# Edge scores: the attributes laid an edge per partition, weighted on VectorE and summed on ScalarE in place of 416 one-column products on PE

## The chip, the cores and the metric

One NeuronCore of a Trainium2 chip runs the whole program. The metric is the device time of one execution in microseconds; before the change it was 3671.51 (median of 3 runs, 3663.25 to 3675.93).

## The reference, cut to what matters

The program is two graph layers, each followed by a mixture of experts, on 3125 nodes with 256 features. The first graph layer scores each of 53,125 edges:

```python
h = x @ Wn.T + bn
e = edge_attr @ We.T + be                # edge_attr: 53125 x 128
a = leaky_relu(sum((h[src] + e) * attn, axis=-1), 0.01)
m = segment_max(a, dst)
a = exp(a - m[dst])
a = a / (segment_sum(a, dst)[dst] + 1e-16)
out = relu(segment_sum(h[src] * a[..., None], dst))
```

By linearity the score before the leaky relu is a sum of three numbers: the source node's `h . attn`, the edge's `edge_attr . (We.T attn)`, and a constant. The change concerns the second: for every edge a dot product of 128 attributes with one fixed vector of 128 weights.

## The kernel before, in words

The kernel runs stage after stage, each in a block of its own in which every engine has its instruction list; a block ends when all engines have. The edges lie in 416 chunks of 128, sorted by destination. The stages are: setup, a layernorm with projection, the sorting of the second layer's edge list (`emit_sort_edges`), **the edge scores** (`emit_edge_scores`, the stage that the change touches), the first aggregation (`emit_aggregate`, tag `a0`), and then experts, second graph layer and second experts.

In the edge-score stage 16 pieces of 26 chunks are worked through, two to a turn of an 8-turn loop, with two buffers `ea` (attributes, 1664 KB a piece) and `lane` (the source node's place in its tile, spread over the partitions, 832 KB).

- SyncE waits until a buffer has been read (`read`) and issues the two transfers of the piece (L295, L296). `read` starts at 2.
- PE, for each piece: two rank products (`rank_tile`, L420 and L421), then 26 products with one column each (L431): a chunk's attributes, attribute per partition and edge per column, are the loaded weights, and the weight vector `we_attn` is the one moving column, so that the chunk's 128 results stand one to a partition in column c of bank 2 of `ps[i]`. In the second piece of a turn another rank tile follows. Then 78 products (L438), three to a chunk, of the one-hot source lanes with the node scores split into three bf16 parts. Each of the 26 products of L431 and each chunk but the last of L438 counts up `step`, the last counts up `mm`.
- VectorE, for each piece: one-hot comparison (L363), one or two rank tiles (L348 to L358, seven small operations), a wait for `mm`, the picking of each edge's tile (L370), its reduction (L374), the addition of bank 2 (L376), and `read`.
- ScalarE has nothing in this stage.
- GpSimd issues 176 indirect scatters (L992, in `Scatter.run`) of another layer's edge records, which have nothing to do with the scores. It is paced: scatter k waits until `step` has come to k x 16 x 51 / 176, less 51. `Scatter.finish` waits at the end of SyncE's list until all scatters have landed.

Before the loop VectorE splits the node scores, releases the buffers and makes the table `tile_hot` (L338); behind it stand the last rank tile and some forty small VectorE operations.

Of the kernel before, what the change touches and what calls it, by code (L numbers as in the profile page):

```python
# [10 lines left out]
F32, BF16, I32, U32 = mybir.dt.float32, mybir.dt.bfloat16, mybir.dt.int32, mybir.dt.uint32  # L11
ALU = mybir.AluOpType
ACT = mybir.ActivationFunctionType
AX = mybir.AxisListType

P = 128
# [9 lines left out]
NC = -(-E // P)  # L26
# [7 lines left out]
ED = 128  # L34
PIECE = 26
NPIECE = NC // PIECE
# [220 lines left out]
def emit_edge_scores(nc, S, A, scatter, rec, rec_dram):  # L257


    sem = S.sem  # L260
    arrived = [sem(f"es_in{i}") for i in range(2)]
    split, hot, mm, step, read = sem("es_split"), sem("es_hot"), sem("es_mm"), sem("es_step"), sem("es_read")
    HALF = PIECE // 2
    with ExitStack() as ctx:
        sb = lambda n, s, d: ctx.enter_context(nc.sbuf_tensor("es_" + n, s, d))
        ea = sb("ea", [P, 2, PIECE * P], F32)
        lane = sb("lane", [P, 2, PIECE * P], BF16)
        onehot = sb("hot", [P, 2, PIECE * P], BF16)
        parts = sb("parts", [P, 3, NT], BF16)
# [5 lines left out]
        trib, onesb = sb("trib", [P, P], BF16), sb("onesb", [P, P], BF16)  # L275
        base = sb("base", [P, NT + 1], F32)
        below, first, last = sb("below", [NB, 2, NT - 1], F32), sb("first", [NB, 1], F32), sb("last", [NB, 1], F32)
        ps = [ctx.enter_context(nc.psum_tensor(f"es_ps{i}", [P, 3, 512], F32)) for i in range(2)]
        psr = ctx.enter_context(nc.psum_tensor("es_psr", [P, 512], F32))
        pst = ctx.enter_context(nc.psum_tensor("es_pst", [P, 512], F32))  # L280
        hots, ranked, tile_read, filled, emptied, listed, counted = (
# [2 lines left out]
        block = ctx.enter_context(nc.Block())  # L284
        lane_row = S.lane_row.rearrange("(a n) -> a n", a=1)

        @block.sync
        def _(sp):
            sp.wait_ge(filled, 1)
            sp.dma_start(rec_dram.rearrange("(p c) r -> p c r", p=P), S.erec_sb[:]).then_inc(emptied, 16)  # L290
            with sp.Fori(0, NPIECE // 2) as o:
                for i in range(2):
                    sp.wait_ge(read, 2 * o + i + 1)
                    col = o * (2 * PIECE * P) + i * PIECE * P
                    sp.dma_start(ea[:, i, :], A["eaT"][:, bass.ds(col, PIECE * P)]).then_inc(arrived[i], 16)  # L295
                    sp.dma_start(lane[:, i, :], lane_row[:, bass.ds(col, PIECE * P)].to_broadcast([P, PIECE * P])  # L296
                                 ).then_inc(arrived[i], 16)

            sp.wait_ge(emptied, 16)
            scatter.finish(sp)  # L300

        @block.gpsimd
        def _(pool):
            nc.gpsimd.memset(S.erec_sb[:, :, 0:1], 0)
            nc.gpsimd.memset(S.erec_sb[:, :, 2:3], 0)
            nc.gpsimd.memset(S.erec_sb[:, :, 1:2], 2 * NP).then_inc(filled, 1)
            issued = itertools.count()
            STEPS = 2 * PIECE - 1

            def pace(pool):  # L310
                steps = next(issued) * NPIECE * STEPS // (scatter.last - scatter.first)
                if steps > STEPS:
                    pool.wait_ge(step, steps - STEPS)

            scatter.run(pool, pace)

        @block.vector
        def _(v):
# [8 lines left out]
            v.drain()  # L327
            nc.vector.tensor_copy(parts[:, 2, :], rest[:, 1, :])
            v.drain().then_inc(split, 1)
            v.sem_inc(read, 2)  # L330

            v.sem_inc(tile_read, 1)
# [13 lines left out]
            def rank_tile(t):  # L346
                v.wait_ge(ranked, t + 1)
                nc.vector.tensor_tensor_scan(incl[:], pst[:, 0:NC], zero[:], 0.0, ALU.add, ALU.add)  # L348
                v.drain()
                nc.vector.tensor_tensor(part[:], incl[:], pst[:, 0:NC], ALU.subtract)  # L350
                nc.vector.tensor_tensor(base[:, bass.ds(t + 1, 1)], base[:, bass.ds(t, 1)], incl[:, NC - 1:NC], ALU.add)
                v.drain()
                nc.vector.tensor_tensor(part[:], part[:], psr[:, 0:NC], ALU.add)
                v.drain().then_inc(tile_read, 1)
                nc.vector.scalar_tensor_tensor(part[:], part[:], base[:, bass.ds(t, 1)], tile_hot[:, bass.ds(t, 1), :].rearrange("p a c -> p (a c)"),
                                               ALU.add, ALU.mult)
                v.drain()
                nc.vector.tensor_tensor(pos[:], pos[:], part[:], ALU.add)  # L358

            with v.Fori(0, NPIECE // 2) as o:  # L360
                for i in range(2):
                    v.wait_ge(arrived[i], 32 * o + 32)
                    nc.vector.tensor_scalar(onehot[:, i, :], lane[:, i, :], S.lane[:, 0:1], None, ALU.is_equal  # L363
                                            ).then_inc(hot, 1)
                    rank_tile(o * 3 + i)
                    if i == 1:
                        rank_tile(o * 3 + 2)
                    v.wait_ge(mm, 2 * o + i + 1)
                    c = o * (2 * PIECE) + i * PIECE
                    nc.vector.tensor_tensor(  # L370
                        picked[:].rearrange("p (a c) t -> p a (c t)", a=2), ps[i][:, 0:2, 0:HALF * NT],
                        S.src_tile[:, bass.ds(c, PIECE), :].rearrange("p (a c) t -> p a (c t)", a=2), ALU.mult)
                    v.drain()
                    nc.vector.tensor_reduce(S.score[:, bass.ds(c, PIECE)], picked[:], AX.X, ALU.add)  # L374
                    v.drain()
                    nc.vector.tensor_tensor(S.score[:, bass.ds(c, PIECE)], S.score[:, bass.ds(c, PIECE)],  # L376
                                            ps[i][:, 2, 0:PIECE], ALU.add)
                    v.drain().then_inc(read, 1)
            with v.Fori(NT - 1, NT) as t:
                rank_tile(t)  # L380
# [31 lines left out]
            keep_visits(nc, v, S, psr, 0, D, S.visit1, S.release1)  # L412
            v.drain()

        @block.tensor
        def _(pe):
            def rank_tile(t):
                pe.wait_ge(tile_read, t + 1)
                counts = tile_hot[:, bass.ds(t, 1), :].rearrange("p a c -> p (a c)")
                nc.tensor.matmul(psr[:, 0:NC], trib[:], counts, start=True, stop=True)  # L420
                nc.tensor.matmul(pst[:, 0:NC], onesb[:], counts, start=True, stop=True).then_inc(ranked, 1)  # L421

            pe.wait_ge(split, 1)
            pe.wait_ge(hots, 1)
            with pe.Fori(0, NPIECE // 2) as o:
                for i in range(2):
                    rank_tile(o * 3 + i)
                    pe.wait_ge(read, 2 * o + i + 1)
                    pe.wait_ge(arrived[i], 32 * o + 32)
                    for c in range(PIECE):  # L430
                        nc.tensor.matmul(ps[i][:, 2, c:c + 1], ea[:, i, c * P:(c + 1) * P], S.we_attn[:, 0:1],  # L431
                                         start=True, stop=True).then_inc(step, 1)
                    if i == 1:
                        rank_tile(o * 3 + 2)
                    pe.wait_ge(hot, 2 * o + i + 1)
                    for c in range(PIECE):
                        for k in range(3):
                            ins = nc.tensor.matmul(ps[i][:, c // HALF, (c % HALF) * NT:(c % HALF + 1) * NT],  # L438
                                                   onehot[:, i, c * P:(c + 1) * P], parts[:, k, :],
                                                   start=(k == 0), stop=(k == 2))  # L440
                        ins.then_inc(step if c < PIECE - 1 else mm, 1)
            with pe.Fori(NT - 1, NT) as t:
                rank_tile(t)
            pe.wait_ge(listed, 1)
            count_visits(nc, pe, S, psr, 0).then_inc(counted, 1)
# [15 lines left out]
def count_visits(nc, pe, S, ps, at):  # L461
    nc.tensor.matmul(ps[0:1, at:at + P], S.ones[0:NB - 1, 0:1], S.passed[0:NB - 1, :], start=True, stop=True)
    return nc.tensor.matmul(ps[0:1, at + P:at + P + NB], S.free[:, 0:1], S.ident[0:NB, 0:NB], start=True, stop=True)
# [1340 lines left out]
```

## Time and profile before

| | |
|---|---|
| median of 3 runs | 3671.51 us |
| profiled execution, its own time | 3665.5 us |
| span in the profile | 3663.7 us |
| PE busy | 2400.6 us, 66% |
| GpSimd busy | 1872.6 us, 51% |
| VectorE busy | 1300.8 us, 36% |
| ScalarE busy | 464.6 us, 13% |
| granted TensorE clock, mean | 0.759 of full |

Times in the rows are microseconds from the span's start, except a mean or a min/median/max, which is in ns. PE is matmul, PEld the loading of its weights, DVE is VectorE, ACT is ScalarE, POOL is GpSimd, SPq the queue of SyncE. "x52" counts instructions that were merged in a row; an fp32 product appears as two. What stands behind "[" is the idle time of that engine before the row, and what ended it; "issue" is a time in which it waited for nothing that the profile shows. Idle time of an engine that is not the bottleneck costs nothing.

### The profile page before, as it was taken

The numbers are of one execution on the slowest core, as the hardware profiler recorded it, in microseconds if no ns is written. First come the engines' busy times: TensorE is split into PE (matmuls) and PEld (weight loads), VectorE is DVE, ScalarE is ACT, GpSimd is POOL, SyncE is SP. The second block draws the span as 40 slices with busy tenths as digits, with TensorE's granted clock in tenths as the row PEclk, the third lists the DMA queues.
The fourth block names the chain that finished last, engine by engine and source line by source line (L and its number), as shares of the span: only waits on it lengthen the run. The fifth ranks groups of instructions, "written<-read, shape, count | busy, mean of one in ns | idle before, by whom it ended". The sixth has DMA issues, their size and how long they took to land. (4 is left out here: it accounts for less than half of the span.)

```text
span 3663.7 us, 38404 instructions
## 1 busy us (share of the span) xinstructions
PE 2400.6 (66%) x10593; PEld 1815.8 (50%) x10594; DVE 1300.8 (36%) x2295; ACT 464.6 (13%) x1252; POOL 1872.6 (51%) x1858
## 2 busy tenths in 40 slices
PE   3239688665555547989899995655555647888800
PEld 3125587543443335667677664443344435666600
DVE  5874444533333343222222224333333241000175
ACT  1126100000000012222222221000000022221100
POOL 0100566466766733666666661777667404665501
PEclk9555555576777767999999998777777758999955
DMA  2102243233333311000000001333333201110001
GB/s 77 37 29 72 101 166 140 79 88 87 91 91 91 92 43 35 12 12 13 13 7 8 12 1 47 90 90 91 90 90 90 69 1 38 20 20 8 8 38 38
DMA packets 121592, 203.86 MB, mean 56 GB/s; under 512 B 55160, under 2 KB 81869, under 8 KB 119117
## 3 DMA queue, kind: packets, MB, share of 16 engines
q0 software_dynamic: 72256, 115.42, 12.5%
q1 hardware_dynamic: 49269, 87.74, 7.1%
q14 instruction: 49, 0.40, 0.0%
q8 instruction: 18, 0.29, 0.0%
HBM read 187.75 MB, written 15.28 MB: 55 GB/s over the span
## 5 line engine op out<-in xcount | busy, mean ns | idle before, releaser
L522 POOL DMA_INDIRECT a1rows<-table,k_esource x416 | 431.9, 1038 | 258.7 <-issue 115.2
L522 POOL DMA_INDIRECT a0rows<-table,k_src x416 | 428.1, 1029 | 219.9 <-issue 112.2
L992 POOL DMA_INDIRECT erecords<-k_rece x416 | 403.1, 969 | 226.8 <-issue 98.1
L594 PE MATMUL a1ps<-a1rows,a1w 128*128 x1024 | 350.9, 505 | 256.0 <-issue 157.6
L594 PE MATMUL a0ps<-a0rows,a0w 128*128 x1024 | 342.9, 497 | 265.9 <-issue 161.7
L594 PEld LDWEIGHTS a1ps<-a1rows,a1w 128*128 128x128 f32 x1024 | 248.1, 253 | 358.7 <-issue 315.8
L594 PEld LDWEIGHTS a0ps<-a0rows,a0w 128*128 128x128 f32 x1024 | 243.8, 249 | 364.9 <-issue 322.3
L992 POOL DMA_INDIRECT records<-k_recg x288 | 298.4, 1036 | 240.5 <-POOLq L898 82.9
L820 PE MATMUL f0up<-k_xnT,f0w 128*128 x1280 | 381.9, 454 | 57.9 <-ACT f0hid L852 24.6
L1329 POOL DMA_INDIRECT gt_land<-table_gat,gt_source x281 | 265.0, 943 | 301.5 <-DVEq L1358 143.5
L830 PE MATMUL f0dn<-f0w,f0hid 128*128 128x256 f32 x1600 | 363.7, 383 | 21.4 <-issue 21.0
L830 PEld LDWEIGHTS f0dn<-f0w,f0hid 128*128 128x128 f32 x1600 | 306.8, 192 | 70.6 <-issue 28.5
L820 PEld LDWEIGHTS f0up<-k_xnT,f0w 128*128 128x128 f32 x1280 | 244.9, 197 | 189.9 <-issue 61.0
L771 DVE SCALAR_TENSOR_TENSOR k_x<-f0dn,k_gate,k_x 128x256 f32 (+1 forms) x200 | 87.2, 480 | 519.3 <-PE f0dn L830 333.2
L852 ACT ACTIVATE f0hid<-f0up,f0b1now 128x384 f32<-128x384 f32 (+1 forms) x320 | 167.8, 527 | 548.3 <-PE f0up L820 390.8
L1556 PE MATMUL f1up<-k_xnT,gt_arena 128*128 x640 | 192.8, 456 | 42.8 <-issue 29.4
L1566 PE MATMUL f1dn<-gt_arena 128*128 128x256 f32 x800 | 188.6, 394 | 18.7 <-issue 11.5
L618 DVE TENSOR_TENSOR k_agg<-k_agg,a1ps 128x256 f32 x128 | 53.9, 421 | 393.4 <-PE a1ps L594 206.8
L618 DVE TENSOR_TENSOR a0acc<-a0acc,a0ps 128x257 f32 x128 | 54.1, 423 | 388.4 <-PE a0ps L594 216.4
L431 PEld LDWEIGHTS es_ps<-k_we_attn,es_ea 128*128 128x128 f32 x832 | 181.8, 333 | 5.9 <-issue 5.7
L1566 PEld LDWEIGHTS f1dn<-gt_arena 128*128 128x128 f32 x800 | 157.3, 198 | 47.6 <-issue 24.9
L431 PE MATMUL es_ps<-k_we_attn,es_ea 128*128 128x1 f32 x832 | 177.9, 349 | 2.6 <-issue 2.5
(438 smaller groups left out, 2582.8 us busy)
## 6 DMA issues: line engine op xcount, KB each, us to landing
es_ea<-in_eaT SPq DMA_DIRECT2D x16, 1664.0 KB
es_lane<-lane_row SPq DMA_DIRECT2D x16, 832.0 KB
so_rowl<-glane_row SPq DMA_DIRECT2D x32, 256.0 KB
a0rows<-table,k_src POOLq DMA_INDIRECT x416
erecords<-k_rece POOLq DMA_INDIRECT x416
a1rows<-table,k_esource POOLq DMA_INDIRECT x416
table<-k_tbl SPq DMA_DIRECT2D x10, 650.0 KB, 3.5
records<-k_recg POOLq DMA_INDIRECT x288
```

Of the source, the lines that this page charges most:

```text
L431: nc.tensor.matmul(ps[i][:, 2, c:c + 1], ea[:, i, c * P:(c + 1) * P], S.we_attn[:, 0:1], start=True, stop=True).then_inc(step, 1)
L522: pool.indirect_dma_start(rows[:, (g + 1) % PLACES, i, :], None, table, bass.IndirectOffsetOnAxis(ap=source[:, c:c + 1], axis=0)).then_inc ...
L594: nc.tensor.matmul(ps[u][:, 0:width], w[:, u // 2, u % 2 * BG + i, :], rows[:, bass.ds(place, 1), i, 0:width].rearrange("p a w -> p (a w)" ...
L618: ins = nc.vector.tensor_tensor(part, part, ps[2 * b + k][:, 0:width], ALU.add)
L771: nc.vector.scalar_tensor_tensor(x_of(j), down[j][:, 0:D], gate_of(j), x_of(j), ALU.mult, ALU.add).then_inc(added, 1)
L820: ins = nc.tensor.matmul(up[q % 2][:, 0:size], w1[:, k, m * P:(m + 1) * P], S.xnT[:, k, bass.ds(g * (U * P) + a * P, size)], start=(k == 0 ...
L830: ins = nc.tensor.matmul(down[j][:, 0:D], hid[half][:, k, (j - a) * P:(j - a + 1) * P], w2[:, k, :], start=(k == 0), stop=(k == KH - 1))
L852: nc.scalar.activation(hid[half][:, m, :], up[q % 2][:, 0:(b - a) * P], ACT.Gelu, bias=bias_now[:, m:m + 1]).then_inc(hid_ready, 1)
L992: pool.indirect_dma_start(self.rec_dram, bass.IndirectOffsetOnAxis(ap=self.rec[:, c + 1, 0:1], axis=0), self.rec[:, c + 1, 1:R], None).the ...
L1329: pool.indirect_dma_start(land[:, j, :], None, S.table_gat, bass.IndirectOffsetOnAxis(ap=source[:, j:j + 1], axis=0)).then_inc(gathered[la ...
L1556: ins = nc.tensor.matmul(up[q % 2][:, 0:size], w1[:, k, m * P:(m + 1) * P], S.xnT[:, k, bass.ds(g * (U * P) + a * P, size)], start=(k == 0 ...
L1566: ins = nc.tensor.matmul(down[j][:, 0:D], hid[half][:, k, (j - a) * P:(j - a + 1) * P], w2[:, k, :], start=(k == 0), stop=(k == KH - 1))
```

## The change

The attributes are laid out by the host with an edge to a partition, chunk after chunk (`ea[:, c, :]` is 128 edges by 128 attributes). The transfers keep their sizes. In a prologue VectorE spreads the weight vector to 128 columns, PE multiplies it with the identity so that every partition holds the whole row, and VectorE copies that row to SBUF. For each piece VectorE first multiplies the 26 chunks in place with the row, ScalarE then runs 26 in-place copies with an accumulator, one to a chunk, into `attr_score`, and VectorE adds that, once `summed` has come. PE's products of L431 and their counting of `step` go, so GpSimd's pacing has 25 steps to a piece and no longer 51.

```diff
+            nc.vector.tensor_copy(we_wide[:], S.we_attn[:, 0:1].to_broadcast([P, P]))
+            v.drain().then_inc(spread, 1)
+            v.wait_ge(spread_done, 1)
+            nc.vector.tensor_copy(we_row[:], psr[:, 0:ED])
             v.sem_inc(read, 2)
...
-            STEPS = 2 * PIECE - 1
+            STEPS = PIECE - 1
...
                     v.wait_ge(arrived[i], 32 * o + 32)
+                    nc.vector.tensor_tensor(ea[:, i, :, :], ea[:, i, :, :], we_row[:].unsqueeze(1).to_broadcast([P, PIECE, ED]), ALU.mult
+                                            ).then_inc(weighted, 1)
                     nc.vector.tensor_scalar(onehot[:, i, :], lane[:, i, :], S.lane[:, 0:1], None, ALU.is_equal
                                             ).then_inc(hot, 1)
...
+                    v.wait_ge(summed, 2 * o + i + 1)
                     nc.vector.tensor_tensor(S.score[:, bass.ds(c, PIECE)], S.score[:, bass.ds(c, PIECE)],
-                                            ps[i][:, 2, 0:PIECE], ALU.add)
+                                            attr_score[:, i, :], ALU.add)
                     v.drain().then_inc(read, 1)
...
+        @block.scalar
+        def _(act):
+            with act.Fori(0, NPIECE // 2) as o:
+                for i in range(2):
+                    act.wait_ge(weighted, 2 * o + i + 1)
+                    act.wait_ge(read, 2 * o + i + 1)
+                    for c in range(PIECE):
+                        ins = nc.scalar.activation(ea[:, i, c, :], ea[:, i, c, :], ACT.Copy, accum_out=attr_score[:, i, c:c + 1])
+                    ins.then_inc(summed, 1)
...
+            pe.wait_ge(spread, 1)
+            nc.tensor.matmul(psr[:, 0:ED], we_wide[:], S.ident[:], start=True, stop=True).then_inc(spread_done, 1)
...
                     pe.wait_ge(read, 2 * o + i + 1)
-                    pe.wait_ge(arrived[i], 32 * o + 32)
-                    for c in range(PIECE):
-                        nc.tensor.matmul(ps[i][:, 2, c:c + 1], ea[:, i, c * P:(c + 1) * P], S.we_attn[:, 0:1],
-                                         start=True, stop=True).then_inc(step, 1)
```

## Rows read from the trace of the kernel before

**Rows 1.** Busy time by stretch: start:end, length, each engine's busy us (instructions), clock, transfers.

```profile
392.50:409.00 16.50, 0.33 (x2) 0.15 (x3) 15.55 (x13) 0.00 (x0) 15.63 (x6) 0.50 0.82 326
409.00:693.60 284.60, 237.14 (x2130) 223.48 (x2128) 130.52 (x210) 0.00 (x0) 175.08 (x174) 0.50 0.35 128
```

**Rows 2.** Instructions of PE in order of time: start, us, what.

```profile
420.29 1.03 PE L438 MATMUL es_ps<-es_parts,es_hot 128*128 128x25 bf16 x33
...
433.43 0.76 PE L438 MATMUL es_ps<-es_parts,es_hot 128*128 128x25 bf16 x22 [0.53 <-issue]
...
480.61 2.54 PE L438 MATMUL es_ps<-es_parts,es_hot 128*128 128x25 bf16 x78
...
495.11 1.53 PE L438 MATMUL es_ps<-es_parts,es_hot 128*128 128x25 bf16 x44
...
502.07 0.75 PE L438 MATMUL es_ps<-es_parts,es_hot 128*128 128x25 bf16 x22 [1.15 <-issue]
502.67 0.51 PE L420 MATMUL es_psr<-es_tilehot,es_trib 128*128 x1
...
503.31 11.09 PE L431 MATMUL es_ps<-k_we_attn,es_ea 128*128 128x1 f32 x52
```

**Rows 3.** The same for VectorE: onehot and rank tile, then picking to the tail.

```profile
505.30 1.08 DVE L363 TENSOR_SCALAR es_hot<-es_lane,k_lane 128x3328 bf16<-128x3328 bf16 x1
...
509.66 0.59 DVE L358 TENSOR_TENSOR es_pos<-es_pos,es_part 128x416 f32<-128x416 f32 x1
...
691.27 0.83 DVE L370 TENSOR_TENSOR es_picked<-es_ps,k_src_tile 128x650 f32<-128x650 f32 x1
...
693.69 1.02 DVE L348 TENSOR_TENSOR_SCAN es_incl<-es_pst,es_zero 128x416 f32<-128x416 f32 x1 [0.34 <-issue]
```

**Rows 4.** The same for GpSimd: the next stage's first gather, and the idle time before it.

```profile
706.59 1.18 POOL L522 DMA_INDIRECT a0rows<-table,k_src  x1 [27.02 <-POOLq L264]
```

**Rows 5.** GpSimd's indirect transfers by line, this stage and the next: busy, mean ns | idle.

```profile
L992 POOL DMA_INDIRECT records<-k_recg x176 | 189.0, 1074 | 96.2 <-issue 33.5 <-PE es_ps L431 31.6 <-PE es_ps L438 30.9
L522 POOL DMA_INDIRECT a0rows<-table,k_src x416: 940/946/2016, 706.6 to 1326.5; - x139
L522 POOL DMA_INDIRECT a0rows<-table,k_src x416 | 428.1, 1029 | 219.9 <-issue 112.2 <-PE a0ps L594 44.7 <-remote 35.9
```

**Rows 6.** VectorE and GpSimd in order of time; the last row by form: count, busy, mean.

```profile
394.50 1.20 POOL L992 DMA_INDIRECT records<-k_recg  x1
397.23 10.96 DVE L338 TENSOR_TENSOR es_tilehot<-k_srct,k_iota 128x10400 bf16<-128x10400 f32 x1
397.28 12.44 POOL L992 DMA_INDIRECT records<-k_recg  x1 [0.31 <-issue]
...
409.85 1.09 DVE L363 TENSOR_SCALAR es_hot<-es_lane,k_lane 128x3328 bf16<-128x3328 bf16 x1 [0.26 <-issue]
410.02 1.74 POOL L992 DMA_INDIRECT records<-k_recg  x1 [0.30 <-issue]
...
1036.77 1.22 DVE L605 TENSOR_TENSOR a0w<-k_iota,a0node 128x1024 f32<-128x1024 f32 x1
1037.06 1.75 POOL L522 DMA_INDIRECT a0rows<-table,k_src  x1 [0.30 <-issue]
L605 DVE TENSOR_TENSOR a0w<-k_iota,a0node 128x1024 f32<-128x1024 f32 x64 | 78.1, 1220 | 0.1
```

**Rows 7.** ScalarE in order of time: sums with an accumulator, then 13 plain ones in SBUF.

```profile
385.32 0.34 ACT L1226 ACTIVATE so_pse<-so_pse,so_minus 128x128 f32<-128x128 f32 x1 [0.81 <-PE so_pse L1210]
385.58 0.19 ACT L1226 ACTIVATION_READ_ACCUMULATOR so_pse<-so_pse,so_minus 128x1 f32 x1
385.67 0.33 ACT L1226 ACTIVATE so_pse<-so_pse,so_minus 128x128 f32<-128x128 f32 x1
...
1334.16 5.29 ACT L727 ACTIVATE a0acc<-a0acc,a0rden 128x256 f32<-128x256 f32 x13 [612.82 <-DVEq L705]
```

**Rows 8.** Transfers by line: KB, us from issue to landing.

```profile
k_w_gcn<-in_gcn_W SPq DMA_DIRECT2D x1, 256.0 KB, 2.6
```

More of the change, by code:

```diff
@@ L262, in emit_edge_scores @@
     split, hot, mm, step, read = sem("es_split"), sem("es_hot"), sem("es_mm"), sem("es_step"), sem("es_read")
+    spread, spread_done = sem("es_spread"), sem("es_spreaddone")
+    weighted, summed = sem("es_weighted"), sem("es_summed")
     HALF = PIECE // 2
@@ L265, in emit_edge_scores @@
         sb = lambda n, s, d: ctx.enter_context(nc.sbuf_tensor("es_" + n, s, d))
-        ea = sb("ea", [P, 2, PIECE * P], F32)
+        flat = sb("ea", [P, 2, PIECE * ED], F32)
+        ea = flat[:].rearrange("p a (c d) -> p a c d", d=ED)
+        we_wide, we_row = sb("wewide", [P, P], F32), sb("werow", [P, ED], F32)
+        attr_score = sb("attrscore", [P, 2, PIECE], F32)
         lane = sb("lane", [P, 2, PIECE * P], BF16)
@@ L277, in emit_edge_scores @@
         below, first, last = sb("below", [NB, 2, NT - 1], F32), sb("first", [NB, 1], F32), sb("last", [NB, 1], F32)
-        ps = [ctx.enter_context(nc.psum_tensor(f"es_ps{i}", [P, 3, 512], F32)) for i in range(2)]
+        ps = [ctx.enter_context(nc.psum_tensor(f"es_ps{i}", [P, 2, 512], F32)) for i in range(2)]
         psr = ctx.enter_context(nc.psum_tensor("es_psr", [P, 512], F32))
@@ L294, in _ @@
                     col = o * (2 * PIECE * P) + i * PIECE * P
-                    sp.dma_start(ea[:, i, :], A["eaT"][:, bass.ds(col, PIECE * P)]).then_inc(arrived[i], 16)
+                    sp.dma_start(flat[:, i, :], A["ea"][:, bass.ds(col, PIECE * ED)]).then_inc(arrived[i], 16)
                     sp.dma_start(lane[:, i, :], lane_row[:, bass.ds(col, PIECE * P)].to_broadcast([P, PIECE * P])
@@ L1785 @@
         "src_pj": padded(src, NC * P, 0).reshape(P, NC), "ew_pc": chunks(edge_weight, NCP),
-        "eaT": np.ascontiguousarray(padded(edge_attr_128, NC * P, 0).T),
+        "ea": padded(edge_attr_128, NC * P, 0).reshape(NC, P, ED).transpose(1, 0, 2).reshape(P, NC * ED),
         "Wn": L0_gnn_Wn, "WnT": np.ascontiguousarray(np.asarray(L0_gnn_Wn).T), "We": L0_gnn_We, "bn": L0_gnn_bn,
```

## The prediction

> **What bounds the kernel now.** I read the page first, then the busy time by stretch, then the edge-score stretch instruction by instruction on each engine. The kernel is a row of stages with a barrier after each, so a change inside one stage is worth what it moves that stage's end. The edge-score stage begins at 392.5 us and the gathers of the next stage begin at 706.6 [rows 1, 4]. The stretch has three parts: a prologue to 409, the loop over 16 pieces of 26 chunks to 693.6 [rows 1], and a tail of small VectorE work from there to 706.0, 12.4 us [rows 3, 4]. In the loop PE is busy 237 of 284.6 us, VectorE 130.5, GpSimd 175.1, ScalarE 0.
>
> On PE, one piece in steady state is 11.1 us for the 26 one-column products (52 records, as an fp32 product is recorded twice), 2.5 us for the 78 one-hot products when they run without gaps and 7.7 us when they have "issue" gaps (495.11 to 502.82), and 0.65 us or twice that for the rank products [rows 2]. The loop's mean is 284.6 / 16 = 17.8 us a piece. The reader is to see that PE starts the next piece's 52 records right behind the last one-hot product (502.07, 502.67, 503.31): PE waits for nothing but itself, and it sets the order of the loop. In its first piece the one-hot part took 13.9 us (420.29 to 434.19), the longest such stretch [rows 2].
>
> VectorE in a piece: onehot and one rank tile from 505.30 to 510.25, so 5.0 us, of which about 4.0 is the rank tile; picking, reduction and addition from 691.27 to 693.69, 2.4 us [rows 3]. There are three rank tiles to two pieces.
>
> GpSimd issues 176 scatters: 189.0 us busy, mean 1074 ns, with 0.30 us between two that wait for nothing [rows 4, 5]. Today it waits for PE's steps in between and still finishes at 706.59 - 27.02 = 679.57, some 26 us before the stage closes [rows 4]. Without its waits it would need 189.0 + 176 x 0.30 = 241.8 us and be done at 394.5 + 241.8 = 636.3 [rows 5, 6]. That is the second bound of this stage, 57 us below PE's loop end. It is the number on which this case hangs.
>
> **The change, part by part.** *Out:* 16 x 11.1 = 178 us of PE. What is left to PE in a piece is 2.5 to 7.7 plus about 1.4, so PE is no longer the bound as long as its gaps stay like that.
>
> *New on VectorE, a multiply of 128x3328 fp32 with a broadcast row, at the head of each piece.* The row of 1024 elements costs 1.22 us, that of 10400 elements 10.96 us [rows 6]: slope 9.74 / 9376, 1.04 ns an element, so 3328 elements cost 1.22 + 2304 x 0.00104 = 3.6 us. Sixteen are 58 us. VectorE then carries 3.6 + 5.0 + 2.4 = 11.0 us in an even piece and 15.0 in an odd one, 208 us in all, below PE's old loop.
>
> *New on ScalarE: 26 sums of 128 elements a piece.* The trace has the same form with an accumulator, from PSUM: start to start 0.35 us (385.32, 385.67), of which the accumulator's read accounts for the last 0.09 [rows 7]. Plain activations in SBUF: 13 of 256 elements in 5.29 us, a pitch of 0.40 [rows 7]. A plain one of 128 elements lies between half of that and all of it, so with the read between 0.29 and 0.49. The upper end for the range is activation and read one after the other, 0.34 + 0.19 = 0.53. I take 0.35, the row with the accumulator, so 9.1 us a piece.
>
> *The new order in a piece.* The sums wait for the multiply, the addition waits for the sums, and the next multiply stands behind that addition on VectorE. So multiply and sums are in series: even piece 3.6 + 0.1 (hand-over) + 9.1 + 0.6 (addition and hand-overs) = 13.4 us, with VectorE's other 7 us hidden beneath the sums; odd piece VectorE's own 15.0, which hides the sums. A pair is 28.4, the loop 8 x 28.4 = 227 us. Queued behind the new wait on VectorE are the addition, the release of the buffer, and the next multiply; the transfers, the sums and PE's next one-hot products wait for those.
>
> *Transfers.* A piece's two transfers are the same bytes as before. Two pieces landed in the 12 to 13 us up to 409 at 326 GB/s mean [rows 1], so one takes about 6.4 us, issued at the release of its buffer one whole piece (13 us or more) ahead: hidden, by about 5 us with a start-up of 2. If that cover were gone, each piece would pay the excess.
>
> *Prologue.* The weight row is spread through PE and copied twice before the buffers are first released: two small copies, one fp32 product and two hand-overs. A rank product takes 0.51 us [rows 2] and the copies no longer than that; I estimate 1.3 us, between 0.5 and 3, all of it in front of the first transfer and of the 10.96 us comparison [rows 6]. The loop begins at 410.3 instead of 409. By VectorE and ScalarE the stage would end at 410.3 + 227 + 12.4 = 650.
>
> *GpSimd's pacing.* It may now be one piece ahead, with 25 steps a piece; 11 scatters a piece need 13.9 us at the free pitch. That is as slow as the new loop, so pacing does not hold it. What does is VectorE. When the 10.96 us comparison ran, a scatter that began 0.05 us after it took 12.44 us; when L363 ran for 1.09 us, a scatter took 1.74; in the next stage, with a L605 comparison begun 0.29 us before it, a gather took 1.75 instead of 0.95, and ended 0.82 us behind the end of L605 [rows 6]. Over that stage the gathers' median is 946 ns and the mean 1029: 416 x 83 ns = 35 us of delay over 64 pairs of L605 and L607, 0.54 a pair [rows 5, 6]. That is what follows if the instruction that meets the operation near its own start stands until the operation ends: on average half a pitch, 0.63 us, of the first operation is already past. (1.22 - 0.63 = 0.6 against the 0.54 seen.) The first case alone could be a full transfer queue, as the transfer engines were busy 82% then [rows 1]; the other two are not. For the new 3.6 us multiply the loss is 3.6 - 0.63 = 3.0 us a piece, 48 us in all, between 0 (no hold) and 3.6 + 1.1 (the onehot behind it holds on, as the copies behind the comparison seem to have done: 12.44 is 0.7 more than 10.96 + 0.82 - 0.05) = 4.7, which is 75 us. I take 48 + 3, as the onehot's hold is partly in today's figure: 189.0 - 176 x 0.96 is 20 us, 11.5 of it the one scatter of the prologue, so 9 us of holds are already counted.
>
> Sum for GpSimd: 636.3 + 51 = 687; then the last scatter has to land before the stage closes, for which I take the 2.6 us of a landing, between 1 and 4 [rows 8]. The stage ends at 690 instead of 706: 16 us saved. VectorE's loop and tail, done at 650, wait beneath it. The next stage is led by its own gathers and moves up as a whole. Against the profiled execution: 3665.5 - 16 = 3649.5; that execution lies 6.0 us under the median of 3671.5, so the measured median should be about 3655.
>
> The row is that an operation with two SBUF inputs held GpSimd's indirect transfers in the next stage [rows 6]. The Trainium skill (SBUF — State Buffer, section "Who interferes with whom") says such an instruction contends with a GpSimd instruction that reads SBUF and not with one that only writes it, and reports that tensor_tensor was not seen to stall descriptor generation. By the first half the forecast stands, as these transfers read their indices in SBUF; by the second the hold would be nothing, which is rival B.
>
> **The rivals.** *B, no hold.* GpSimd ends at 636 and the stage at VectorE's and ScalarE's 650: 56 us saved, 3615. For it: the longest hold, 12.44 us, coincides with busy transfer engines, and nothing in this stage shows a hold by such an operation beside idle ones. Against it: the two short holds of [rows 6].
> *C, ScalarE becomes the bound, and the kernel slower.* If activation and accumulator read run one after the other in SBUF, the pitch is between 0.34 + 0.19 = 0.53 and 0.40 + 0.19 = 0.59, and the stage ends 7 to 31 us late. At 0.54 a piece is 3.6 + 0.1 + 14.0 + 0.6 = 18.3 us, the loop 293, the stage's end 716, 10 us late: 3682. It decides from the pitch where 410.3 + 16 x piece + 12.4 = 706, which is a piece of 17.7 us, a pitch of 0.51. Against it: [rows 7] show the overlap.
> *D, PE's gaps or a middle pitch.* With gaps in both pieces a PE-led piece is 3.6 + 1.1 + 7.7 + 2.4 = 14.8 us, still hidden by GpSimd; with ScalarE at 0.47 a piece is 16.5 us and the stage ends at 687, too. With some of both, or GpSimd's hold at its upper end (636.3 + 75 + 2.6 = 714 less today's own holds of about 9, so 705), the gain is 0 to 16 us: 3664. With gaps as in the first piece always (13.9 us), a piece would be 21 us and the kernel 50 us slower; every later piece speaks against that.
>
> **How the numbers follow.** GpSimd-led forecast 0.52 (own range 3644 to 3664), B 0.17, C with the always-gapped PE 0.13, D 0.18. A measurement of this kernel tells from no change about 0.3%, 11 us. Faster: B whole, 0.44 of the forecast's 0.52 and 0.05 of D: 0.66. Same: 0.20, out of the forecast's small end and D. Slower: C and a remnant, 0.14. The range reaches to B's value and to half-way into C: 3612 to 3678. Predicted: 3655.
>
> **What would show it.** In the changed kernel's profile: the scatters' mean rises from 1074 to about 1360 ns ((189.0 + 51) / 176), with one of 3 to 5 us in each piece beside the multiply; the last scatter ends near 687 and VectorE has been idle for some 35 us before the stage closes; ScalarE's sums start 0.35 us apart; the multiply lasts 3.6 us; PE is idle most of each piece. Wrong, if the scatters stay at 0.96 us (B), if VectorE's longest wait is for the sums in both pieces and the last scatter is done long before (C), or if PE's one-hot products are what the picking waits for (D).

## The result and the profile after

The changed kernel takes 3742.74 us (median of 4 runs, 3740.28 to 3749.37) against 3670.91 for the kernel before (4 runs, one more than when the forecast was made, 3663.25 to 3675.93): a ratio of 1.020, 95% interval 1.0178 to 1.0223. The forecast was 3655 in a range of 3612 to 3678, most likely faster. It is 2% slower.

The profiled execution took 3740.28 us with a span of 3738.5, so 74.8 us more than the span before. All of it is in the edge-score stage. GpSimd's first gather of the next stage, and the idle time before it:

```profile
781.98 1.18 POOL L543 DMA_INDIRECT a0rows<-table,k_src  x1 [27.65 <-POOLq L266]
```

It came at 706.59 before [rows 4], so the stage ends 75.4 us later, where 16 us earlier was forecast. Busy time by stretch (columns as in [rows 1]), the second being the loop:

```profile
393.00:411.00 18.00, 1.65 (x4) 0.64 (x4) 16.48 (x16) 0.00 (x0) 16.94 (x7) 0.50 0.79 310
411.30:767.00 355.70, 67.52 (x1296) 45.13 (x1296) 184.43 (x222) 123.28 (x832) 196.11 (x172) 0.50 0.28 101
```

PE went from 237 to 68 us in the loop, as meant, yet the loop grew from 284.6 to 355.7 us and no engine is busy for much more than half of it. So it is a chain of waits. What was waited for, in total, times, longest:

```profile
ACT es_ea L435 <- DVE es_ea L373: 250.3, 16, 23.2
...
DVE es_picked L382 <- remote: 122.5, 12, 11.2
PE es_ps L459 <- DVE es_hot L375: 116.4, 8, 17.7
...
DVE es_picked L382 <- PE es_ps L459: 30.2, 2, 15.8
```

ScalarE waits for the multiply, PE for the one-hot comparison behind it, and VectorE's picking for PE (`mm`); "remote" is where the profile could name no releaser. One piece of VectorE, in order of time:

```profile
509.92 3.63 DVE L373 TENSOR_TENSOR es_ea<-es_ea,es_werow 128x3328 f32<-128x3328 f32 x1 [0.45 <-issue]
513.46 1.08 DVE L375 TENSOR_SCALAR es_hot<-es_lane,k_lane 128x3328 bf16<-128x3328 bf16 x1
...
517.82 0.59 DVE L368 TENSOR_TENSOR es_pos<-es_pos,es_part 128x416 f32<-128x416 f32 x1
527.66 0.83 DVE L382 TENSOR_TENSOR es_picked<-es_ps,k_src_tile 128x650 f32<-128x650 f32 x1 [9.25 <-remote]
528.66 0.83 DVE L386 TENSOR_REDUCE k_score<-es_picked 128x650 f32 x1 [0.16 <-issue]
529.57 0.18 DVE L389 TENSOR_TENSOR k_score<-k_score,es_attrscore 128x26 f32 x1
529.87 3.62 DVE L373 TENSOR_TENSOR es_ea<-es_ea,es_werow 128x3328 f32<-128x3328 f32 x1
```

PE in the same piece:

```profile
514.69 2.10 PE L459 MATMUL es_ps<-es_parts,es_hot 128*128 128x25 bf16 x73 [17.69 <-DVE es_hot L375]
517.13 0.21 PE L459 MATMUL es_ps<-es_parts,es_hot 128*128 128x25 bf16 x2 [0.34 <-issue]
517.87 0.22 PE L459 MATMUL es_ps<-es_parts,es_hot 128*128 128x25 bf16 x2 [0.53 <-issue]
518.64 0.18 PE L459 MATMUL es_ps<-es_parts,es_hot 128*128 128x25 bf16 x1 [0.55 <-issue]
519.36 0.50 PE L443 MATMUL es_psr<-es_tilehot,es_trib 128*128 x1 [0.53 <-issue]
520.10 0.51 PE L444 MATMUL es_pst<-es_tilehot,es_onesb 128*128 x1 [0.24 <-issue]
```

The reader is to lay these two side by side. All 78 products are recorded by 518.8, 4.3 us after the comparison is done; the picking, which waits for nothing but the last of them, starts at 527.66. The trace also holds when each semaphore was counted up. For this piece:

```
comparison done 514.55
step (one a chunk)  514.94 515.02 515.10 to 515.82 (12 counts, 0.08 apart)
                    517.09 517.87 520.06 521.50 524.33 525.79
                    527.22 527.27 527.32 527.37 527.42 527.47
mm                  527.52      rank product recorded at 520.10: counted 527.56
GpSimd's scatters   515.76, then one each 1.26 to 1.7 us up to 525.07; the next at 527.96
```

Counts come every 0.08 us until the first scatter, from then on mostly at multiples of some 0.72 us, and in the pause after the eighth the rest comes at once, 0.05 us apart. The products themselves had run ahead. (One count of the 26 has no record.) From the comparison's end to `mm` it takes 13.0 us in one piece of a turn and 18.7 in the other, 15.1 on average over the 16 (in the second piece of a turn some 3 us of it are PE's wait for VectorE's first rank tile, which has to be read before PE's second); multiply and comparison are 4.7, picking to the next multiply 2.4. Sum 22.2; the 15 steps from `mm` to `mm` measured 21.9 each. That is the loop.

### The profile page after: what moved, and what is told of

Read it like the earlier page. It is cut to its first block and busy times, and to the rows that moved or that the text cites. A ratio compares the mean times of both kernels' runs of the same rounds, so it can differ in the third digit from the quotient of the medians.

```text
span 3738.5 us, 37636 instructions
## 1 busy us (share of the span) xinstructions
PE 2230.3 (60%) x9763; PEld 1631.4 (44%) x9764; DVE 1359.2 (36%) x2313; ACT 588.4 (16%) x2084; POOL 1889.6 (51%) x1858
## 5 line engine op out<-in xcount | busy, mean ns | idle before, releaser
L1013 POOL DMA_INDIRECT records<-k_recg x288 | 320.3, 1112 | 293.7 <-POOLq L919 82.9
L1577 PEld LDWEIGHTS f1up<-k_xnT,gt_arena 128*128 128x128 f32 x640 | 124.4, 201 | 110.9 <-issue 49.0
L435 ACT ACTIVATE es_ea<-es_ea 128x128 f32<-128x128 f32 x416 | 121.8, 294 | 250.3 <-DVE es_ea L373 250.3
```

Of the source, the lines that this page charges most:

```text
L435: ins = nc.scalar.activation(ea[:, i, c, :], ea[:, i, c, :], ACT.Copy, accum_out=attr_score[:, i, c:c + 1])
L1013: pool.indirect_dma_start(self.rec_dram, bass.IndirectOffsetOnAxis(ap=self.rec[:, c + 1, 0:1], axis=0), self.rec[:, c + 1, 1:R], None).the ...
L1577: ins = nc.tensor.matmul(up[q % 2][:, 0:size], w1[:, k, m * P:(m + 1) * P], S.xnT[:, k, bass.ds(g * (U * P) + a * P, size)], start=(k == 0 ...
```

## The experiments

Where a stage's end is given it is the first gather of the next stage (706.6 before, 782.0 changed). Several chips were used; on some the kernel before took 3632 to 3634 us where it took 3665 to 3671 on others, so total times are compared only with the kernel before on the same chip, and the rest by the traces. Where no number of runs is given there was one.

**The order of the chain, the loop of PE, the number of products.** Theory G: GpSimd's scatters make PE's short products slow to arrive. Theory S: PE's instructions are supplied too slowly, in the form tested here because of the loop's jumps. The kernel before took 3664.54 us on this chip.

```diff
@@ onehot_first: comparison ahead of the multiply
-    multiply; onehot
+    onehot; multiply
@@ pe_written_out (and the same of the kernel before)
-            with pe.Fori(0, NPIECE // 2) as o:
+            for o in range(NPIECE // 2):
@@ one_product: leaves out two of the three bf16 parts of the node scores
-                        for k in range(3):
+                        for k in range(1):
```

> The changed kernel with VectorE's one-hot comparison ahead of the multiply in each piece. Theory S (supply): PE's 78 one-hot products of a piece take 13.0 or 18.7 us from the comparison's end to the last count, because PE's instructions come too slowly once the first dozen chunks are through; this stands in series with the multiply, the comparison and the picking. Then the multiply (3.6 us) leaves the chain: a turn of two pieces is 46 - 7 = 39 us, the kernel some 58 us faster than the changed one, near 3685. Rival A (ScalarE's sums are the chain): the sums start later by 1.1 us a piece, so 18 us slower than the changed one, 3760.

Measured 3670.78 us, stage end 708.9: 73 us of the 75 lost are back, more than expected. The 3.6 us of the multiply now lie beside PE's products, and that is not all: in the first piece of each turn the time from comparison to `mm` fell to 2.4 to 4.4 us, while in the second it stayed long (12.9 to 24.0, mostly 19.6). In the piece whose comparison ends at 488.6 the 78 products run from 488.76 to 491.16 and `mm` comes at 491.17, while the multiply holds GpSimd's scatter:

```profile
489.04 3.95 POOL L1013 DMA_INDIRECT records<-k_recg  x1 [0.30 <-issue]
```

There the addition waits 2.2 us for ScalarE's sums instead. So in the changed kernel it is the chain through PE that sets the loop.

> The changed kernel with PE's 8-turn loop written out (8 turns of instructions one behind the other, no jump back). Theory S, in the form that the jump back is what makes PE's instructions come late: comparison to last count falls from 13.0 and 18.7 us to 3 us, the loop is then led by multiply and sums (28 us a turn) and the stage ends with GpSimd's last scatter, near 687: about 3655. If the slow supply has nothing to do with the jump (each piece of new code is late the first time): no change or slower, 3740 to 3840. Rival W (the count-ups of PE's products are what is slow): unchanged, 3740.

> The kernel before with PE's 8-turn loop written out. Theory S with the jump back as its cause: the one-hot products take 2.3 us in every piece instead of 7 to 8, a turn is 2 x (11.1 + 2.3) + 3 x 0.65 = 29 us instead of 34 to 35, and the stage ends near 655: 50 us faster than before, 3620. If the jump is not the cause: 3670 or slower. Rival W: unchanged, 3670.

Measured 3752.09 (stage end 787.4) and 3667.23 (706.6). From comparison to `mm` the pieces are 13.0 and 18.7 us with PE's loop written out, as with the loop. S falls in the form that the jumps are the cause.

> The changed kernel with one product to a chunk instead of three: the second and third bf16 part of the node scores are left out, so the scores are coarser; PE has 26 products a piece instead of 78, with the same 26 count-ups. Theory S: the first 36 or so products of a piece run without a gap today, so all 26 do: comparison to last count about 1 us and the kernel near 3655, led by GpSimd. Rival W (count-ups are slow): the count-ups are as many, so 13.0 and 18.7 us stay, 3740. Rival T (transfers slow the supply): between, a third of the stretch, 4 to 6 us, and still led by GpSimd near 3660.

Measured 3698.49, stage end 734.4: between the theories. With a third of the products, one piece of a turn had its 26 counts within 0.9 us and the other still took 19 to 22 (the last 7.7). The slow piece was again the one with scatters beside it; the number of products alone does not set it.

**Scatters, their number and their kind.** Here the kernel before took 3632.56 us. `EARLY` is the number of the 288 scatters that lie in this stage; the others move to the experts' stage, which grows, so the totals say nothing and the stage's end is what is read.

```diff
@@ few_scatters (of the changed kernel, and of the kernel before)
-EARLY = 176
+EARLY = 8
@@ memsets: 8 scatters, and at the same pace
+            for _ in range(168):
+                pace(pool)
+                nc.gpsimd.memset(scratch[:], 0.0)     # 128 x 640 f32
+                pool.drain()
@@ one_sum: leaves out the edge part of 25 of 26 chunks
-                    for c in range(PIECE):
+                    for c in range(1):
                         ins = nc.scalar.activation(...)
```

> The changed kernel with 8 instead of 176 of the scatters in the edge-score stage; the other 168 go to the experts' stage, which has 112 + 416 of them already. Theory S (PE's instructions come late behind the jump back) is refuted by the written-out loop, which kept every stretch to 0.1 us. New theory G: PE's short products run slowly (0.7 us and multiples of it from count to count) only while GpSimd issues indirect transfers beside them. Then comparison to last count is 3 us or less in all pieces, a turn is 12 + 15 = 27 us, and the next stage's gathers begin near 645 instead of 782; the whole kernel 3600 if the experts' stage hides the 168, up to 3740 if it does not. Rival D (data transfers of the piece slow PE) or rival W (PE's counts themselves): still 13.0 and 18.7 us, gathers at 782.

Measured 3786.71; stage end 637.2, that is 145 us earlier. From comparison to `mm` it is 2.4 and 5.5 us in all 16 pieces (the 5.5 holds the wait for a rank tile). The gather:

```profile
637.20 1.18 POOL L543 DMA_INDIRECT a0rows<-table,k_src  x1 [58.00 <-POOLq L266]
```

> The kernel before with 8 instead of 176 scatters in the edge-score stage. Theory G: the one-hot products take 2.2 us in each piece, a turn 2 x (11.1 + 2.2) + 3 x 0.65 = 29 us, gathers of the next stage near 655 instead of 706. Rivals D and W: 706.

Measured 3809.22; stage end 656.0. The same 168 scatters cost the stage before 706.6 - 656.0 = 50.6 us, 0.30 each, and the changed one 145, 0.86 each. With 8 scatters the change is worth 19 us; with 176 it costs 75.

> As the changed kernel with 8 scatters, and in the place of the other 168 a GpSimd memset of about 1 us each, at the same pace: GpSimd is as busy, and issues no transfers. Theory G in the form that the transfers (their descriptors, packets and counts) slow PE: PE as fast as without, gathers at 645. In the form that a busy GpSimd or its waits on PE's count slow PE: gathers near 780.

Measured 3792.43; stage end 638.0, pieces 2.4 and 5.5 us (the first 5.5). GpSimd was busy in bursts at the same places, and nothing slowed:

```profile
499.64 5.88 POOL L325 MEMSET es_scratch<- 128x640 f32 x8
512.16 8.12 POOL L325 MEMSET es_scratch<- 128x640 f32 x11 [6.64 <-PE es_ps L464]
```

So it is the indirect transfers, not that GpSimd works.

> The changed kernel with one sum a piece on ScalarE instead of 26; 25 of 26 chunks miss the edge's part of their score. Every theory in which PE's one-hot products are the chain (G, D, W): the sums end at 521.3 where the picking starts at 527.7, so no change, 3742. Rival C of the prediction (the sums are the chain): 3742 less 16 x 7.3 = 3625.

Measured 3698.1, 1.018 of the kernel before as the changed kernel's 1.020; stage end 762.3, and 13.7 us from comparison to `mm`. Taking away 7.3 of ScalarE's 7.6 us a piece gives back 20 of the 75 us: rival C (ScalarE the bound) falls, which had 117. But nothing had been expected to come back. The 20 us are there because `mm` comes sooner, mostly 14.3 for 18.7 us in the second piece of a turn; why fewer ScalarE instructions make PE's counts come sooner is not shown.

**Ordering one piece ahead, no pacing, transfers by another engine.** The kernel before took 3633.79 us here.

```diff
@@ onehot_ahead: the comparison of piece p + 1 in piece p
+            onehot_of(0, 16)
             per piece:
                 multiply(i)
-                onehot(i)
+                onehot_of(1 - i, ...)      # gated by the lane transfer alone
                 rank tiles; wait mm; pick; reduce; wait summed; add
@@ unpaced (of the changed kernel, and together with onehot_ahead)
-                if steps > STEPS:
-                    pool.wait_ge(step, steps - STEPS)
@@ sync_transfers: EARLY = 8, and SyncE issues 176 small transfers
+                    for j in range(11):
+                        sp.dma_start(S.probe[... P rows ...], S.lane[:, 0:1]).then_inc(probed, 16)
```

> The changed kernel, with each piece's one-hot comparison made one piece ahead on VectorE, so that PE's one-hot products of the next piece no longer stand behind the multiply and the comparison of that piece. Theory G (the loop is the chain multiply, comparison, slow products, picking; the products cost 13.0 and 18.7 us because GpSimd issues scatters beside them): PE runs without a break, a piece costs some 15 to 16.5 us, the loop ends at 650 to 675 and GpSimd's scatters with their holds decide the stage's end at about 690 (next stage's first gather; 782 in the changed kernel, 706.6 before): about 0.4% faster than the kernel before. Rival, that a piece is slow because the scatters stretch with PE's work in it (PE slower still when GpSimd has more scatters per us): the products grow to 18 us or more each, gather at 710 to 730, no gain over before.

Measured 3638.18 us (10 runs), ratio 1.001, interval 0.999 to 1.003; stage end 714.2. The 2% are back, no more. The rival's number came: a piece costs 18.9 us on average (`mm` at 414.0 to 697.0, 15 steps). But PE does not work without a break. The steps are 4.5 to 6.2 us and 27 to 36 us in turn (557.82, 563.77, 593.42; the last 18.8), and in the long one PE waits for VectorE's first rank tile, behind which stands its own second:

```profile
579.45 0.52 PE L459 MATMUL es_psr<-es_tilehot,es_trib 128*128 x1 [10.82 <-DVEq L367]
```

That rank tile stands behind the multiply on VectorE (572.33 to 575.96), and the 78 products behind PE's rank products, from 580.11 on, with their last count at 593.42. So in every second piece PE's products were still in series with the multiply, and the slow counts with them; a version with the rank tile ahead too was not run. The last scatter begins at 692.7, 1297 ns on average:

```profile
L1029 POOL DMA_INDIRECT records<-k_recg x176 | 228.3, 1297 | 71.4 <-issue 49.2 <-PE es_ps L475 22.1
```

> The changed kernel with 8 scatters instead of 176, and 176 small transfers of 128 elements of 4 bytes, each to its own row of DRAM, issued by SyncE, 11 to a piece. If the transfers' traffic slows PE's short products, comparison to last product stays at 13 to 19 us and the gather comes near 780. If it is GpSimd's own issuing of an indirect transfer, it is 2.4 and 5.4 us as with few scatters, and the gather comes at about 640.

Measured 3813.52; stage end 660.7, comparison to `mm` 2.4 and 5.5 us throughout. (The 23 us above 637 are waits for the lane transfer, 26.2 us in 7 times, which stands behind the small ones in SyncE's queue.) Transfers of 128 small pieces issued by SyncE do nothing of the kind: it is something that goes with GpSimd's indirect ones. Whether that is GpSimd's issuing or the way in which such transfers then run is not told apart, as no direct transfer was issued by GpSimd.

> The changed kernel, with GpSimd's scatters no longer waiting for PE's steps. If each scatter costs PE its 0.86 us wherever it falls, the stage ends where it did, gather at 782. If a scatter costs PE only when short products are under way, the scatters that now fall beside VectorE's multiply and picking cost nothing, and once they are all out (at about 690) the pieces run at 13 us: gather at about 740.

> The last kernel, and GpSimd's scatters no longer wait for PE's steps. If the sum of slow stretches is a price per scatter (0.86 us each in the changed kernel), nothing changes against the last kernel: gather at about 690, decided by GpSimd (241.8 us of pitch and some 50 us of holds from 394.5). If the waits on PE's steps were costing GpSimd time, the gather comes earlier, down to 660.

Both expectations failed, and these runs show most of the mechanism. Measured 3791.16 and 3770.01 (4 runs, ratio 1.0389, interval 1.0359 to 1.0418), stage ends 858.6 and 846.3. In the first the scatters run one each 1.26 us to 635, and up to 657 no more than two pieces are done. PE in the unpaced kernel, first and second piece:

```profile
430.61 0.26 PE L459 MATMUL es_ps<-es_parts,es_hot 128*128 128x25 bf16 x3 [1.22 <-issue]
432.00 0.51 PE L443 MATMUL es_psr<-es_tilehot,es_trib 128*128 x1 [1.14 <-issue]
...
502.65 1.00 PE L459 MATMUL es_ps<-es_parts,es_hot 128*128 128x25 bf16 x30
504.21 0.18 PE L459 MATMUL es_ps<-es_parts,es_hot 128*128 128x25 bf16 x1 [0.57 <-issue]
507.01 0.18 PE L459 MATMUL es_ps<-es_parts,es_hot 128*128 128x25 bf16 x1 [2.61 <-issue]
...
511.92 0.18 PE L459 MATMUL es_ps<-es_parts,es_hot 128*128 128x25 bf16 x1 [2.61 <-issue]
```

VectorE there, where the first piece is picked:

```profile
492.45 0.83 DVE L382 TENSOR_TENSOR es_picked<-es_ps,k_src_tile 128x650 f32<-128x650 f32 x1 [71.86 <-remote]
```

GpSimd meanwhile, two of 176 alike:

```profile
458.92 0.95 POOL L1013 DMA_INDIRECT records<-k_recg  x1 [0.30 <-issue]
460.18 0.96 POOL L1013 DMA_INDIRECT records<-k_recg  x1 [0.30 <-issue]
```

ScalarE in the second piece, from its tenth sum on:

```profile
500.95 0.29 ACT L435 ACTIVATE es_ea<-es_ea 128x128 f32<-128x128 f32 x1
501.15 0.19 ACT L435 ACTIVATION_READ_ACCUMULATOR es_ea<-es_ea 128x1 f32 x1
502.10 0.31 ACT L435 ACTIVATE es_ea<-es_ea 128x128 f32<-128x128 f32 x1 [0.76 <-issue]
503.50 0.20 ACT L435 ACTIVATION_READ_ACCUMULATOR es_ea<-es_ea 128x1 f32 x1 [1.10 <-issue]
504.89 0.31 ACT L435 ACTIVATE es_ea<-es_ea 128x128 f32<-128x128 f32 x1 [1.19 <-issue]
```

The last product of the first piece is recorded to end at 430.9, when 15 chunks of 26 have been counted, and the picking starts at 492.45. `step` is counted at 458.70, 467.11, 475.50, 483.90 and `mm` at 492.31: 8.40 us for three products, 2.80 each, long after they ran. In the second piece 31 products run within 1.7 us behind two rank products, and then one each 2.80 us. ScalarE runs ten sums at 0.29 us, and then one instruction each 1.40, the read counted as one. The reading, which fits all these times but was not tested by itself: each engine's instructions report their end through something that holds a limited number (some 33 products on PE, in both pieces, ten sums on ScalarE), and while GpSimd issues indirect transfers it empties slowly, in the end 2.80 us a product and 1.40 us an instruction of ScalarE. It is not that slow at once: up to 444.71, some 50 us into the stream, a whole chunk of three products was counted mostly each 2.8 us (435.54, 438.35, 441.19). Why it slows further is not shown. First the count-ups lag; when it is full, the engine stands. When GpSimd has paused it empties at once, with counts 0.05 us apart: in the changed kernel 1.2 us after the scatter before had ended (527.22), in the unpaced one, after 176 scatters without a pause, only 21 us after (656.83).

**Short products alone? More scatters early?** The kernel before took 3632.67 us here.

```diff
@@ before_unpaced: the pacing wait out of the kernel before
@@ before_200, ahead_200: the kernel before and onehot_ahead
-EARLY = 176
+EARLY = 200
```

> The kernel before, and GpSimd's scatters no longer wait for PE's steps. Theory F (while GpSimd issues scatters without a break, instructions reach the other engines only one at a time, one each 1.4 us, whatever they do; in the changed kernel without the waits both PE's products of 2.8 us and ScalarE's sums showed it): PE's long one-column products are starved as well, no longer 0.43 us apart but up to 2.8, and the stage ends later than without scatters being unpaced: gather at 830 or later instead of 706.6. Rival (only short products suffer): the one-column products stay 0.43 us apart, the scatters are out at about 640, and the gather comes at 706 or before.

Measured 3800.4; stage end 875.7. The long one-column products starve as well:

```profile
500.53 0.16 PE L431 MATMUL es_ps<-k_we_attn,es_ea 128*128 128x1 f32 x1 [2.64 <-issue]
503.33 0.16 PE L431 MATMUL es_ps<-k_we_attn,es_ea 128*128 128x1 f32 x1 [2.64 <-issue]
506.13 0.16 PE L431 MATMUL es_ps<-k_we_attn,es_ea 128*128 128x1 f32 x1 [2.64 <-issue]
```

These are 2.80 us for each record. A whole fp32 product is two, and `step` is counted every 5.60 us (599.92, 605.52, 611.12), twice what theory F gave; before, it was 0.43. F's stage end came, but its mechanism (instructions delivered late) does not stand: the count-ups of the unpaced changed kernel come up to 61 us behind products that have run, which late instructions can't do.

> The kernel before, with 200 of the 288 scatters in the edge stage instead of 176, and 24 fewer in the experts' stage. By the price of a scatter in the edge stage before (0.30 us) and in the experts' stage (1.23 us): 7 us more and 30 us less, some 22 us faster than before (ratio 0.994). Rival: below today's number the experts' stage is bound by PE (731 of 799 us busy) and gets nothing back: 7 us slower or more.

Measured 3634.23 us (10 runs), ratio 1.0007, interval 0.9983 to 1.0031. The edge stage ends 33 us later (739.2) and the experts' stage is 33 us shorter (758 us, for 791 in the unpaced kernel before on the same chip, whose experts' stage is the same as before's): the edge stage pays 1.36 us for each further scatter, not 0.30, so the 0.30 was a mean over a stage in which most were free.

> The kernel with the comparison made one piece ahead, with 200 scatters in the edge stage instead of 176. There a scatter costs more, (714.2 - 637) / 168 = 0.46 us: 11 us more in the edge stage and, by the price of the experts' stage, 30 us less: 18 us faster than the kernel with 176. Rival: GpSimd had no room left in this stage (last scatter at 693 of 714), each further one costs its 1.3 us, 31 us, and nothing is gained.

Measured 3643.91 us (10 runs), ratio 1.0037, interval 1.0022 to 1.0052; stage end 745.4, again 31 us later, as the rival said. No version that was tried beats the kernel before.

## Why the prediction was wrong

**The step that failed** is "What is left to PE in a piece is 2.5 to 7.7 plus about 1.4, so PE is no longer the bound as long as its gaps stay like that." The term measured 15.1 us, from the comparison's end to the last count. It was taken from the recorded durations of the products [rows 2], and the gaps in them were taken for PE's own; with 8 scatters the kernel before has none, and its 78 products take 2.2 to 2.3 us in every piece. But what VectorE waits for is the count-up, and the rows of before already parted the two. After "480.61 2.54 ... x78" [rows 2], which ends at 483.15, the picking started at:

```profile
488.51 0.83 DVE L370 TENSOR_TENSOR es_picked<-es_ps,k_src_tile 128x650 f32<-128x650 f32 x1 [3.70 <-remote]
```

That is 5.4 us behind the last product; in the changed kernel with few scatters the count comes with the last product's recorded end (525.06 and 525.05). The lag cost nothing before: PE had gone on with the 11.1 us of the next piece's one-column products, which do not depend on the picking. The removed products were the cover of this lag. Rival D had the mechanism's outline ("a piece would be 21 us and the kernel 50 us slower"), and "every later piece speaks against that" dismissed it by the recorded durations, and left such a case a part of the 0.13. With 15.1 its sum is 4.7 + 15.1 + 2.4 = 22.2 a piece, 16 x 22.2 = 355 for the loop (355.7 measured), and with the forecast's own prologue and tail the stage's end comes 72 us late (75 measured).

**The chain.** The forecast had multiply and sums in series, and PE beside them. The multiply also stands ahead of the one-hot comparison, so PE's products are in series with it, too; rival D's sum had that, the forecast's did not. Moving the comparison alone gave 73 us back.

**The multiply, the sums, the prologue** were right: 3.63 us (forecast 3.6), a pitch of 0.29 us (forecast 0.35, lower end 0.29), the first piece 1.5 us later (forecast 1.3). In the changed kernel ScalarE is never the bound.

**GpSimd held by the multiply** was right in kind and too dear in sum. The multiply of the first piece, on VectorE:

```profile
411.33 3.63 DVE L373 TENSOR_TENSOR es_ea<-es_ea,es_werow 128x3328 f32<-128x3328 f32 x1 [0.26 <-issue]
```

The scatters beside it and beside the prologue's comparison:

```profile
398.89 12.31 POOL L1013 DMA_INDIRECT records<-k_recg  x1 [0.30 <-issue]
411.50 4.58 POOL L1013 DMA_INDIRECT records<-k_recg  x1 [0.30 <-issue]
```

A scatter begun 0.17 us after the multiply stood until 1.1 us behind its end (the comparison follows right behind); another, begun 0.6 us after one, took 4.12. The Trainium skill (SBUF — State Buffer, "Who interferes with whom") has such a VectorE instruction contend with what GpSimd reads; the trace agrees with that half, and not with its report that this operation did not stall them. In all, the scatters took 211.6 us for 189.0, mean 1202 ns, 22.6 us of holds and not 51: in many pieces GpSimd was itself waiting for PE's counts when the multiply ran. Rival B (no hold) is wrong, but that hold decided nothing of the 75 us.

**GpSimd's bound of 636** was right: unpaced, the last scatter began at 635.1 and ended at 636.1. But the stage was never bound by it, as the same scatters are what slows PE. The forecast added the loads of the engines side by side and had no term for what one does to another.

**Left open.** What the reports go through is not shown. The starts in the unpaced kernel are 2.1, 2.8 or 3.5 us apart on PE (507.01 to 509.13, 539.22 to 542.71) and once 0.7 on ScalarE, so multiples of some 0.70 us. Four such units to a product and two to an instruction of ScalarE would fit a start and an end record for each weight load, product and instruction, though not the faster counts before 444.7. The Trainium skill (NOTIFIC — the notification-queue block, "Interfaces") says that the block which writes such records can hold back an engine "when a queue is full in FORENSIC mode or an internal FIFO fills". No run here tells the recording apart from the count-up itself, and all times given here are of executions whose instructions were recorded; whether the 2% remain where nothing is recorded is not shown. Why a scatter costs 0.86 us in the changed loop, 0.46 with the comparison ahead ((714.2 - 637.2) / 168, its own few-scatter end not being measured) and 1.36 at the margin of before is told by overlap, not by a rule that was tested.

## What to carry to other kernels

Read a product's cost where its waiter starts, or at its count-up, and not where its record ends; if the two are apart and nothing is lost by it, something covers the difference, and the change may remove the cover. Before work is taken off an engine, look at what its successor waits for and put the new work behind, not ahead of, what feeds the slow partner. Beside a stream of GpSimd's indirect transfers, many small instructions on PE and ScalarE were dear here, and letting the stream run free cost 77 us of the stage in the changed kernel and 169 in the one before: try such a stream paced before it is tried free.

## What the runs showed of the hardware

Some 50 us into a stream of GpSimd's indirect transfers back to back (one each 1.26 us), PE got one recorded product done each 2.80 us, whether bf16 with 25 columns or one of the two records of an fp32 product with one column, and ScalarE one instruction each 1.40 us; without them they take 0.03, 0.21 and 0.15 us. The same number of GpSimd memsets, or of 128-piece transfers issued by SyncE, does nothing of the kind. Removing a pacing wait, which only takes a restriction away, made the kernel before 4.6% slower (one run, 3800.4 for 3632.67).
